# Two-layer gated cross-attention: score tiles taken by head group, key maxima as full-array products, and value products in bursts of six key tiles

## The reference

```python
x = x + tanh(g_xattn[0]) * xattn0(layernorm(x), ctx, ctx, ..., mask)      # 64 experts, top 8 behind it
x = x + tanh(g_ffn[0])   * moe0(layernorm(x), ...)
x = x + tanh(g_xattn[1]) * xattn1(layernorm(x), ctx, ctx, energies, ...)  # 8 experts, top 2 behind it
x = x + tanh(g_ffn[1])   * moe1(layernorm(x), ...)
# xattn: scores = q @ k.T / sqrt(8); layer 0 masks with where(mask, scores, min)
#        attn = softmax(scores); layer 1 multiplies attn by sigmoid((mean|energy| - 0.1) * 10) per key
#        out = (attn @ v) @ Wo + bo
```

## Time and profile before

| | |
|---|---|
| time, median of 3 runs (lowest to highest) | 1043.95 us (1043.92 to 1044.07) |
| the profiled execution | 1045.04 us, of which the trace's span is 1043.2 us |
| PE / DVE / ACT / POOL busy, share of the span | 87% / 72% / 56% / 30% |
| layer 0: first exp; batch 7's last score taken | 76.6 us; about 416 us |
| layer 1: first score; attention's end | 623.2 us; about 929 us |

### The profile page before, as it was taken

How to read it: one execution, slowest core, us unless ns; L and a number is a source line. 1 busy time by engine, 2 the same in 40 slices (tenths; PEclk the granted TensorE clock), 3 DMA queues, 4 the chain that set the end, 5 groups by cost and what they waited for, 6 DMA issues and landing times.

```text
span 1043.2 us, 24614 instructions
## 1 busy us (share of the span) xinstructions
PE 910.7 (87%) x9812; PEld 631.8 (61%) x9812; DVE 750.1 (72%) x1420; ACT 579.4 (56%) x1214; POOL 310.1 (30%) x276
## 2 busy tenths in 40 slices
PE   4569899999999989589998669999999999967996
PEld 3125566666666666478887325665666566646885
DVE  6676776776767735679997885788778777216996
ACT  2305556656556576356665214776777676654664
POOL 2610302113021110057776320421422331002774
PEclk8558999999999999689999655999999999686999
DMA  6670314132240410076671640324414412104651
GB/s 153 117 166 2 81 36 116 31 87 69 49 115 2 87 32 2 9 188 180 184 198 49 135 112 1 83 63 88 112 35 87 116 24 65 33 1 118 165 166 52
DMA packets 49016, 88.91 MB, mean 85 GB/s; under 512 B 22169, under 2 KB 32605, under 8 KB 48901
## 3 DMA queue, kind: packets, MB, share of 16 engines
q1 hardware_dynamic: 48900, 87.34, 34.2%
HBM read 47.32 MB, written 0.65 MB: 46 GB/s over the span
## 4 chain that ended last, share of the span: by engine, by line
PE 62%; DVE 14%; ACT 9%; POOL 6%; issue 5%; DMA 3%; SPq 1%; POOLq 0%; DVEq 0%; ACTq 0%
PE ps L1181 20%; PE po L1202 16%; PE pm L1151 9%; POOL tmpf L785 6%; ACT probs L861 5%; PE ps L1185 4%; PE pc L1116 4%; PE pc L1129 4%; DVE qsel L538 3%; DVE vaug L547 3%; ACT qsel L955 3%; DVE mx_part L434 2%; DVE junk L437 1%; PE pm L1290 1%; DVE junk L441 1%
## 5 line engine op out<-in xcount | busy, mean ns | idle before, releaser
L861 ACT ACTIVATE probs<-ps 121x400 f32<-121x400 f32 (+1 forms) x768 | 356.5, 503 | 209.9 <-PE ps L1185 125.3
L1181 PE MATMUL ps<-qst,kst 128*121 128x400 f32 (+3 forms) x768 | 318.2, 460 | 29.6 <-ACT probs L861 28.1
L434 DVE TENSOR_REDUCE mx_part<-pm 100x2 f32<-100x964 f32 x192 | 213.7, 1158 | 64.6 <-PE pm L1151 64.6
L1181 PEld LDWEIGHTS ps<-qst,kst 128*121 128x121 f32 (+3 forms) x768 | 141.8, 189 | 145.2 <-ACT probs L861 89.9
L437 DVE CUSTOM_DVE_ANT_0 junk<-pm,negq 100x964 bf16<-100x964 f32 x128 | 143.5, 1158 | 55.2 <-PE pm L1151 55.2
L1202 PE MATMUL po<-probs,vaug 121*32 121x100 f32 x6144 | 179.0, 259 | 1.5 <-ACT probs L861 1.5
L1290 PE MATMUL pm<-qsel,qst 128*128 128x400 f32 x660 | 158.3, 364 | 16.1 <-DVE qsel L538 12.1
L1202 PEld LDWEIGHTS po<-probs,vaug 121*32 121x32 f32 x6144 | 135.0, 113 | 54.8 <-ACT probs L861 32.0
L1151 PE MATMUL pm<-khi,qbd 32*100 32x482 f32 x768 | 128.5, 488 | 37.1 <-DVE mx_part L434 13.8
L1290 PEld LDWEIGHTS pm<-qsel,qst 128*128 128x128 f32 x660 | 122.6, 196 | 34.8 <-DVE qsel L538 33.9
L785 POOL TENSOR_TENSOR tmpf<-vaug,wb 128x400 f32<-128x400 f32 x55 | 68.6, 1247 | 195.6 <-DMA wb<-routing 138.3
(11 more groups left out here) (179 smaller groups left out, 893.1 us busy)
## 6 DMA issues: line engine op xcount, KB each, us to landing
kst<-khi SPq DMA_DIRECT2D x128, 180.5 KB, 3.9
wb<-routing SPq DMA_DIRECT2D x102, 200.0 KB, 3.7
ctxT<-in_ctxT SPq DMA_DIRECT2D x16, 722.0 KB, 4.3
kst<-klo SPq DMA_DIRECT2D x64, 180.5 KB, 3.9
wts<-in_experts SPq DMA_DIRECT2D x55, 192.0 KB, 3.7
qsel<-qhi SPq DMA_DIRECT2D x16, 100.0 KB, 2.3
kst<-kst SPq DMA_DIRECT2D x7, 180.5 KB, 3.6
wb<-routing SPq DMA_DIRECT2D x4, 300.0 KB, 3.6
```

Of the source, the lines that this page charges most:

```text
L434: ins = nc.vector.tensor_reduce(parts[:, 2 * i:2 * i + 2, j, x], bank, AX, ALU.max)
L861: nc.scalar.activation(probs[t % 2][0:r, g * GQ:(g + 1) * GQ], ps[0:r, n % 2, 0:GQ], ACT.Exp, scale=SCALE).then_inc(s["probs_ready"], 1)
L1181: mm = nc.tensor.matmul(ps[0:r, n % 2, 0:GQ], kst[b % 2][0:rows, g, t * KEY_TILE:t * KEY_TILE + r], qst[b % 2][0:rows, g * GQ:(g + 1) * GQ ...
```

## The change

Attention runs by **steps**, 48 to a batch: one head group's 12 key tiles, then the next group's. A step is one score product and one exp; a slot of before is four steps' work.

- Four score banks `ps` (step n uses bank n % 4) and two single banks `pm` for the maxima. A score waits for the exp four before it.
- Maxima are full-array products: 13 tiles of 125 rows (the 100 queries of one head, and 25 of one of the three heads that are left) with all 128 contraction rows, three chunks of 482 keys each, so 39 products per batch. DVE takes each by itself (one reduce of 482 columns), and product i waits until the one two before it is taken. 17 run ahead of a layer's first score, 31 more in the first 24 steps, and then 39 per 48 steps.
- The row maxima come in four pieces per batch (one per head group), with a transpose, an ACT copy and one or two DMAs each. `ROW_AT` puts them at steps 28 and 43 of the batch before and at 10 and 14 of the batch itself.
- Value products run in bursts of six key tiles, 24 products, every sixth step (n % 6 = 3); `probs` is a ring of 18.
- `kst` is a ring of five head-group stacks, three DMAs each; SP issues the row of batch 0 ahead of the stacks of later batches.
- The output products stand at steps 6, 9 and 12, key chunks at 20, 24 and 28, value chunks at 34, 37 and 40. `pc_free` chains the users of `pc`: each waits for whoever read the one before.
- Layer 0's masks for the maxima (`negq`, now four arrangements) are made by ACT; its energies come in one DMA; the mask's transposed part is made earlier on POOL. The MoE's second product uses banks of `ps` in place of `pm`.

```diff
-QUADS_AHEAD = 2
-ROW_SLOT = QUADS - QUADS_AHEAD
-TURN_OUT_SLOT, TURN_BACK_SLOT, OUT_SLOT, K_SLOT, V_SLOT = 1, 2, 3, 4, 7
+MAX_TILES, BLOCK = 13, 25
+MAX_ROWS = S + BLOCK
+MAXES = MAX_TILES * 3
+MAX_TILES_OF = [(0, 4), (4, 8), (8, 12), (12, 13)]
+SCORE_BANKS = 4
+KST_RING = 5
+PROBS = 18
+VALUES_PER, VALUES_AT = KEY_TILES // 2, SCORE_BANKS - 1
+MAX_FIRST, MAX_EARLY, EARLY_STEPS = 17, 31, 24
+TURN_OUT_AT, TURN_BACK_AT, OUT_AT = 6, 9, 12
+SECOND_K_AT, K_AT, V_AT = [2, 7, 11], [20, 24, 28], [34, 37, 40]
...
+                def take_max(i):
...
+                    dve.wait_ge(s["chunk_ready"], i + 1)
+                    bank, lo = pm[0:MAX_ROWS, i % 2, 0:MAX_W], MAX_STARTS[c]
...
+                        ins = nc.vector.tensor_reduce(mx_part[0:MAX_ROWS, m, c:c + 1], bank, AX, ALU.max)
+                    ins.then_inc(s["max_taken"], 1)
...
+                def max_product(i):
...
+                    if i >= 2:
+                        pe.wait_ge(s["max_taken"], i - 1)
+                    nc.tensor.matmul(pm[0:MAX_ROWS, i % 2, 0:MAX_W], qbd[b % 2][:, m, :],
+                                     khi[b % 2][:, MAX_STARTS[c]:MAX_STARTS[c] + MAX_W], start=True, stop=True)\
+                        .then_inc(s["chunk_ready"], 1)
...
-                    if n >= 2:
-                        pe.wait_ge(s["probs_ready"], n - 1)
+                    if n >= SCORE_BANKS:
+                        pe.wait_ge(s["probs_ready"], n - SCORE_BANKS + 1)
...
+                def max_rows(b, c):
+                    pe.wait_ge(s["rowmax_ready"], b * G + c + 1)
+                    pc_free(("mrow_ready", b * G + c + 1))
...
+                def at_step(n):
+                    b, x = divmod(n, STEPS_PER)
+                    scores(n)
+                    if n % VALUES_PER == VALUES_AT and n >= VALUES_PER:
+                        weigh(*divmod(n // VALUES_PER - 1, 2))
+                    for i in range(maxes_before(n), maxes_before(n + 1)):
+                        max_product(i)
...
-                for k in range(QUADS):
-                    max_quad(0, k)
...
+                for i in range(MAX_END[0, 0]):
+                    max_product(i)
+                max_rows(0, 0)
+                for i in range(MAX_END[0, 0], MAX_FIRST):
+                    max_product(i)
+                for n in range(STEPS):
+                    at_step(n)
...
-                stack(l, 1, 1)
-                row(l, 0)
-                context(l, 3, 1)
+                row(l, 0, 0)
+                for n in range(STEPS):
+                    b, x = divmod(n, STEPS_PER)
+                    if n in ROW_AT:
+                        row(l, *ROW_AT[n])
...
```

More of the change, by code:

```diff
@@ L242, in flamingo @@
         wts = [sb(f"wts{i}", [128, 3, 128]) for i in range(RING)]
-        wb = [sb(f"wb{i}", [128, TOK]) for i in range(RING)]
+        shared = sb("shared", [128, RING * TOK])
+        wb = [shared[:, i * TOK:(i + 1) * TOK] for i in range(RING)]
+        mask_u = over(shared, 0, [128, 4, NK], U8)
+        own = PROBS - RING * TOK // GQ
+        probs = [sb(f"probs{i}", [KEY_TILE, GQ]) for i in range(own)] + \
+            [over(shared, i * GQ, [KEY_TILE, GQ]) for i in range(PROBS - own)]
         sg = [over(tmpf, v * HALF, [128, HALF]) for v in range(2)]
@@ new lines, in max_rows, with scores @@
+                def max_rows(b, c):
+                    pe.wait_ge(s["rowmax_ready"], b * G + c + 1)
+                    pc_free(("mrow_ready", b * G + c + 1))
+                    nc.tensor.transpose(pc[:, 0:MAX_ROWS], rowmax[0:MAX_ROWS, :], ident[0:MAX_ROWS, 0:MAX_ROWS])\
+                        .then_inc(s["maxrow_ready"], 1)
+                def scores(n):
+                    b, x = divmod(n, STEPS_PER)
+                    (g, t), u, bank = divmod(x, KEY_TILES), n // KEY_TILES, n % SCORE_BANKS
+                    r = rows_of(t)
+                    if l == 0 and n == 0:
+                        pe.wait_ge(pool_init, 10)
+                        pe.wait_ge(ones_ready, 1)
+                    if l == 0 and n == KEY_TILES:
+                        pe.wait_ge(rows_spread, (KST_RING - 1) * 16)
+                    if n == 2:
+                        pe.wait_ge(s["vraw_ready"], 2)
+                    if t == 0:
+                        pe.wait_ge(s["kstack_in"][u % KST_RING], (u // KST_RING + 1) * 48)
+                        pe.wait_ge(s["qstack_ready"], u + 1)
+                        for c in (range(G) if g == G - 1 else (g,)):
+                            pe.wait_ge(s["mrow_in"][c], (b + 1) * ROW_MOVES[c])
+                    if n >= SCORE_BANKS:
+                        pe.wait_ge(s["probs_ready"], n - SCORE_BANKS + 1)
@@ L1198, in weigh @@
                             pe.wait_ge(s["oraw_ready"], b)
-                    for g in range(G):
+                    for t in range(half * VALUES_PER, (half + 1) * VALUES_PER):
+                        r = rows_of(t)
                         for j in range(J):
@@ L1279, in attention @@
+                for i in range(MAX_END[0, 0], MAX_FIRST):
+                    max_product(i)
+                for n in range(STEPS):
+                    at_step(n)
+                weigh(UNITS - 1, 1)
                 turn_out(B - 1)
@@ L1399, in context, with stack @@
                     .then_inc(s["ctx_in"][par], 16)
-            def stack(l, b, par):
+            def stack(l, u):
                 s = A[l]
+                b, g = divmod(u, G)
                 sp.wait_ge(s["klo_ready"], b * 3 + 3)
-                if not (isinstance(b, int) and b < 2):
-                    sp.wait_ge(s["pv_done"], b * KEY_TILES - KEY_TILES)
-                for g in range(G):
-                    for i, part in enumerate((khi, klo, khi)):
-                        sp.dma_start(kst[par][32 * i:32 * i + 32, g, :].bitcast(F32),
-                                     part[b % 2][32 * g:32 * g + 32, :].bitcast(F32)).then_inc(s["kstack_in"][par], 16)
```

568 lines of the change are left out of this document (262 added, 306 removed).

## The result

The changed kernel takes 1083.25 us (median of 4 runs, 1082.15 to 1084.43) against 1044.01: a ratio of 1.0376, 95% interval 1.0356 to 1.0397. It is slower, on the side that was forecast and inside the range, but by 39 us where 16 were forecast. The profiled execution took 1082.15 us, its span 1080.3.

The account below looks back on a forecast made before the run. TensorE's list was taken to bound the middle of attention. Shorter starts (-20, -26) and batch 7 (-7.9, +0.5) against longer batch 0 (+6.8, +10) and middles (+19.9, +33.0) gave +16.3, so 1060 us; range 1006 to 1095.

Parts of the forecast that it names:

- The cycle: Six attention steps on TensorE, from burst to burst: 4.25 us in layer 1 and 4.5 in layer 0.
- The bank loop: At the maxima, product, DVE take and next product take 1.21 us per bank, 0.61 per maximum with two banks.
- The waits at `pc`: TensorE waits for DVE: 1.2 to 1.3 us at step 10, 1.3 at 14, 1.0 at chunk 24, 1.2 at 28.
- The periods: Middle batches grow to 43.2 us in layer 1 from 37.2, and to 46.4 in layer 0 from 42.35.
- TensorE's own work: TensorE's products per middle batch without waits: 34.0 us in layer 1, 40.1 in layer 0.
- the starts: First scores come earlier with a shorter SP queue: -20 us in layer 1, -26 in layer 0 (bounds 20 to 30).
- 3.4 us ahead of the first score: Layer 1's start before: SP's row issued at 619.78, first score at 623.2; used to place the new first score.
- The signs: Right if first score nears 603, first exp 50, periods are 42 to 44.5 and 45 to 48, `pc` waits over 1 us.
- the waits in full: Upper bound on middle batches: 45 us in layer 1, 48.5 in layer 0; slower case's own range 1046 to 1085.
- That the waits hide: Rival: ACT's four banks and earlier takes hide middle waits; 1007 us at old periods, 1034 half hidden; chance 0.29.
- That the clock falls in the middle: Rival: TensorE's waits lower its clock, costing 4 us per middle batch, about 1105 us; chance 0.12.
- the rule on row-tiled products: Skill's four row-tiled products ran 3.07 times as fast as sequential ones, speaking against giving up quads for the maxima.

Follow-up runs that it names:

- (7): Changed kernel with DVE's answers to `pc` users ahead of the same step's take, and those users spread over more steps: 1048.27 us, ratio 1.0000 to the kernel before.
- (1): Changed kernel with its six banks split three for scores and three for maxima: 1059.44 us, ratio 1.0115 to the kernel before.
- experiment 11: Changed kernel with three maxima banks, answers first, row ahead of the stacks, and `pc` users spread one step further: 972.71 us, ratio 0.9237 to the kernel before.
- Experiment 5: Changed kernel with batch 0's row issued behind the second stack, ahead of later stacks, energies, mask rows and context: 1071.17 us, ratio 1.0220 to the kernel before.
- 2: Changed kernel with three score banks and two for maxima, one bank idle, as a control: 1089.47 us, ratio 1.0398 to the kernel before.
- experiment 4: Changed kernel with value products in bursts of three key tiles in place of six: 1100.26 us, ratio 1.0510 to the kernel before.
- experiment 6: Changed kernel with the mask's transposed part made later on POOL, behind batch 0's score queries: 1085.62 us, ratio 1.0351 to the kernel before.
- 3: Changed kernel with DVE's answers to the users of `pc` put ahead of the same step's take: 1048.12 us, ratio 1.0009 to the kernel before.
- 8: Changed kernel with three maxima banks, answers first, `pc` users spread and row ahead of the stacks: 987.69 us, ratio 0.9421 to the kernel before.
- 9: Changed kernel with DVE taking only the last 64 of each maximum's 482 columns: 1013.49 us, ratio 0.9626 to the kernel before.
- 10: Changed kernel with three maxima banks, answers first and row ahead of the stacks, without spreading `pc` users: 1005.70 us, ratio 0.9551 to the kernel before.
- 12: The fastest version (experiment 11) with value bursts of three key tiles: 995.17 us, ratio 0.9508 to the kernel before.

## Why the prediction was right and wrong

*The cycle and the waits: right.* The bank loop gave 4.25 us per plain cycle and gives 4.25. The waits at `pc` were forecast at 1.2 to 1.3, 1.3, 1.0 and 1.2; in the batch shown step 10 waits 1.30, key chunk 24 0.97 and the transpose at 28 1.30. Three runs show that these waits are the loss: shorter takes alone give 70 us back, answers first 35, a third bank 24 to 30. (The text ahead of the prediction counts one wait on DVE's takes per slot of before; its own rows show two, so 24 per batch became 39.) They are not independent: a wait taken away at `pc` came back at the maxima as long as two banks held (7), and one taken away at the maxima grew at `pc` (1).

*The periods, the first step that failed: 43.8 and 47.1 where 43.2 and 46.4 were counted.* (The pieces listed add up to 43.3 and 46.6.) Mis-sized was TensorE's own work, counted at 34.0 and 40.1. In experiment 11, where few waits are left, the same products take 36.8 and 41.3, with TensorE busy 244.3 of 244.6 us in layer 0 and 211.9 of 216.7 in layer 1, so the own work is some 36.0 to 36.8 and 41.3. Then the waits of the changed kernel are 7.0 to 7.8 us per batch in layer 1 and 5.8 in layer 0, where 9.2 and 6.3 were counted: own work too short and waits too long nearly cancel, and that the periods came within 0.7 us is in part luck. Small prices were missing: a score stands 0.32 behind a maximum that had waited (766.83 to 767.15 in the changed kernel's list) or that followed a burst (765.59 to 765.92), and 0.22 behind another (766.10 to 766.32); a burst begins 0.27 behind the score ahead of it (768.75 to 769.02 on the same timeline), not 0.18. With eight bursts per batch these come to about 1.5 us, an estimate. In the sum, 0.6 to 0.7 us in ten plain batches is 6.5 of the 8.8 us by which the middle was short; most of the rest is one batch in each layer that ran 1.2 and 1.5 us longer with the clock low for a time (below).

*The second step that failed: the starts, -46 forecast, -37.6 measured.* "3.4 us ahead of the first score" was taken from a row that SP issued over 2 us behind the last stack's DMA. Right behind stacks and a context it took 5.4 in layer 1 (617.32 to 622.76), which is the whole miss of 1.9 there, and 8.5 in layer 0, where it took 4.5 before:

```profile
71.13 0.52 SPq L1418 DMA_DIRECT2D qst<-mrow  x1
```

```profile
75.65 0.66 PE L1181 MATMUL ps<-qst,kst 128*121 128x400 f32 x1 [0.20 <-DMA qst<-mrow]
```

Experiment 5 shows that place alone to be worth 12 us. Layer 0's list also began 4.6 us late (first stack 25.77, before 21.21): SP stood 6.74 us at one DMA of the mask, before 3.68, and that this comes from the mask's broadcast copies ahead of it was only argued. From the first stack to the row the list is 28.0 us shorter (21.9 for 49.9), where 23.6 was counted from the DMAs that leave it; 28.0 less 4.6 and less 4.0 for the row's landing is the 19.5 measured, just outside my bounds of 20 to 30.

*The signs.* The periods, the waits of about 1 us and more, and a clock of 0.99 in the middle came as the signs of being right had it. Layer 0's first exp came at 57.1, not near 50. Layer 1's first score came at 622.8, not near 603, because layer 0 ended later; measured from the MoE's first product it is 18.1 us earlier than before.

*The forecast as a difference.* It was +16 out of about +70 of losses and -54 of gains. Misses of 8.8 us in the middles' 53 and of 8.4 in the starts' 46, both to the same side, with 3.6 elsewhere (2.9 of it in layer 1's batch 7), more than double it. That is what made a right mechanism a wrong size; the range took it in, since it went by the waits in full.

*The rivals.* That the waits hide: not here, but it is what the list does once DVE's answers come in time. With most waits short the middle is a little below before (41.3 and 36.8 against 42.35 and 37.2). Of the 72.9 us between the span of before and that of experiment 11 the two starts make 56.0 and the middles 15.8. So the full-array products and bursts save TensorE little; the smaller stacks, the pieces and the row's place let each layer begin sooner, and of these only the row's place was tried by itself. That the clock falls in the middle: a small part, shown by rows below. What the rule on row-tiled products made of the maxima can't be told apart in these runs.

## What to carry to other kernels

Where one engine works through a list and another answers, what matters is the order within the answering engine's step: put the answer that is waited for ahead of the work that only fills. Take waits away together: one alone may only move to the next place, and a change that looks worthless by itself (spreading, with two banks) can be worth 18 us beside another. The time from a small transfer's issue to the work that waits for it depended here on what was queued ahead of it (8.5 or 2.5 us), so take its price from a row in the same place of the queue. A forecast that is a small difference of large terms needs each term's error beside it, and a sum that comes out right can hold two errors that cancel.

## What the runs showed of the hardware

**The clock fell behind a wait at `pc`, in some batches.** Three windows in turn from one batch of layer 1 of the changed kernel (columns as in the earlier trace rows):

```profile
788.30:790.30 2.00, 0.54 (x3) 0.14 (x1) 1.80 (x3) 0.77 (x2) 0.00 (x0) 1.00 0.00 0
790.30:794.20 3.90, 3.87 (x9) 2.63 (x10) 1.01 (x2) 1.83 (x5) 0.00 (x0) 0.56 0.00 1
794.20:796.00 1.80, 1.80 (x51) 1.32 (x51) 1.50 (x3) 0.93 (x3) 0.00 (x0) 1.00 0.00 0
```

After TensorE was busy 0.54 of 2.0 us (the wait at step 28) the granted clock is 0.56, near the lower level of 1.2 GHz, over a window of 3.9 us, and the batch is 45.0 us long, its neighbours 43.8 and 44.2. The same wait in the neighbours leaves the clock at 1.00. The changed kernel and experiments 1, 2, 4, 5 and 6, which keep the waits of over 1 us at `pc`, have one to four such falls in their twelve middle batches, and each of these batches is 1.0 to 1.9 us longer than the plain ones; in experiments 3 and 7 to 12, whose waits there are mostly shorter, the middles show 1.00 throughout. Why one wait brings a fall and the next doesn't, no run shows. The Trainium skill ("TensorE: Matmul & The Clock Gate", A second HAM failure mode: psum-queue depth-cycling) tells of a kernel that cycles PSUM banks and whose clock turns so often that it costs throughput; this trace has such turns, but only one in the middle of each layer.

In layer 1's batch 7 the clock was 0.77 before, 0.95 in the changed kernel and 0.65 in experiment 4. The 11 us of experiment 4 there go with the clock (TensorE busy 41.6 us, 28.8 in the changed kernel); why it stood low these runs don't explain. How much of the changed kernel's 5 us is the clock's and how much the score banks' isn't separated either.

**Some small DVE operations stand still while POOL holds a large one.** In the changed kernel the product of two small tiles takes 2.67 us, before 0.26; it ends at 21.99, POOL's operation (17.67, 4.26 long) at 21.93:

```profile
19.32 2.67 DVE L407 TENSOR_SCALAR any_diag<-ident,any_q 100x100 f32<-100x100 f32 x1
```

```profile
17.67 4.26 POOL L784 TENSOR_SCALAR negT<-maskT_u 121x1200 bf16<-121x1200 uint8 x1 [9.22 <-DMA maskT_u<-in_maskT]
```

In experiment 6, with POOL idle there, the same line takes 0.26. Not every DVE operation is caught: a reduction that ran into the same POOL operation took 1.66 us, as long as in experiment 6.

```profile
17.50 1.66 DVE L404 TENSOR_REDUCE any_q<-shared 100x1 f32<-100x1444 uint8 x1 [0.88 <-DMA maskT_u<-in_maskT]
```

What sets the two apart was not tried. The Trainium skill ("SBUF — State Buffer", Terms) says that the two share a pair of ports that one holds for a whole instruction while the other is blocked; the 2.67 us, ending 0.06 behind POOL's operation, agree.
